# Adaptive-norm mixture of experts on one core: where the shared expert begins, who adds its residual, how fast the bit search is paced, and how the logits are made

## The reference, cut to what matters

```python
x = L0_attn_x                                  # (2, 2048, 128) float32, 4096 tokens
mod = (silu(L0_c) @ L0_wmod)                   # sa, ca, ga, sb, cb, gb; |ga|, |gb| at least 0.25
h = layernorm(x) * (1 + ca) + sa
x = x + ga * causal_mean(h)                    # running mean over the tokens of a sequence
h = layernorm(x) * (1 + cb) + sb
# ffn on xf = h as (4096, 128); E = 8 experts, F = 512
scores = softmax(xf @ gate_weight.T).T
vals, idx = top_k(scores.reshape(-1), 8192)    # over all experts and tokens together
gate = zeros((8, 4096)).at[idx // 4096, idx % 4096].add(vals)
y = gelu(xf @ W1[e] + b1[e]) @ W2[e] + b2[e]   # for each expert e
shared = gelu(xf @ Ws1 + bs1) @ Ws2 + bs2
out = x + gb * (sum over e of gate[e] * y[e] + shared)
```

## Time and profile before

| | |
|---|---|
| median of 3 runs | 421.06 us |
| profiled execution | 420.8 us, span 419.0 us |
| TensorE matmul busy | 293.0 us (70%) |
| VectorE | 181.8 us (43%) |
| ScalarE | 142.0 us (34%) |
| POOL (GpSimd) | 217.3 us (52%) |

### The profile page before, as it was taken

One profiled execution on the slowest core, in us unless ns is written; L12 is line 12 of the kernel. 1 busy time (PEld: TensorE's weight loads), 2 busy tenths in 40 slices (PEclk: granted clock), 3 DMA queues, 4 the chain that ended last, 5 costly groups with the idle time before them and its releaser, 6 DMA issues.

```text
span 419.0 us, 5097 instructions
## 1 busy us (share of the span) xinstructions
PE 293.0 (70%) x1182; PEld 165.6 (40%) x1182; DVE 181.8 (43%) x790; ACT 142.0 (34%) x228; POOL 217.3 (52%) x208
## 2 busy tenths in 40 slices
PE   1256676677899869799977878776798676895000
PEld 1144463444445446365544335444344443342000
DVE  0578989615666665534542343442243341121100
ACT  1014455465445432254423332233333223341000
POOL 0122523300111213655788778887778887756662
PEclk9999868657999996699989898898989889899555
DMA  8573322011011002935455554555544555323321
GB/s 241 144 196 96 106 77 75 25 52 13 0 39 39 25 27 55 280 85 166 84 114 121 122 110 62 102 122 120 118 91 88 99 122 118 69 26 30 31 27 18
DMA packets 50463, 37.04 MB, mean 88 GB/s; under 512 B 7879, under 2 KB 44542, under 8 KB 50430
## 3 DMA queue, kind: packets, MB, share of 16 engines
q0 software_dynamic: 13824, 14.46, 20.3%
q1 hardware_dynamic: 36368, 21.78, 18.3%
q10 hardware_dynamic: 238, 0.42, 0.3%
HBM read 24.70 MB, written 11.94 MB: 87 GB/s over the span
## 4 chain that ended last, share of the span: by engine, by line
issue 47%; POOL 31%; DMA 10%; PE 6%; DVE 2%; POOLq 1%; SPq 0%; ACT 0%; DVEq 0%
POOL out_dram L854 19%; POOL R L841 7%; DMA out_dram<-R,IDXB 4%; DMA R<-rows_scratch,IDXB 4%; PE U L942 2%; PE Y L962 2%; POOL SM L821 2%; POOL ACC L874 2%; DMA out_dram<-OUT 1%; DVE GJ L719 1%; PE R L907 1%; POOL SM L815 1%; DMA CST<-in_consts_dram 1%; PE R L1050 1%; POOL SM L823 1%
## 5 line engine op out<-in xcount | busy, mean ns | idle before, releaser
L854 POOL DMA_INDIRECT out_dram<-R,IDXB x72 | 113.2, 1572 | 34.6 <-issue 20.4
L841 POOL DMA_INDIRECT R<-rows_scratch,IDXB x72 | 70.2, 975 | 32.8 <-issue 19.1
L354 ACT ACTIVATE HF<-U,CB 128x512 f32<-128x512 f32 x72 | 49.5, 687 | 99.0 <-PE U L942 80.2
L962 PE MATMUL Y<-HF,WU 128*128 128x512 f32 x144 | 81.7, 655 | 0.0
L942 PE MATMUL U<-XT,WU 128*128 128x512 f32 x144 | 77.5, 620 | 0.7 <-issue 0.7
L907 PE MATMUL R<-CST,R 128*128 128x128 f32 x128 | 25.9, 337 | 41.2 <-DMA R<-rows_scratch,IDXB 36.7
L762 DVE SCALAR_TENSOR_TENSOR R<-R1b,GT,R 128x128 f32<-128x128 f32 x72 | 20.4, 344 | 66.3 <-PE R1b L907 37.7
L942 PEld LDWEIGHTS U<-XT,WU 128*128 128x128 f32 x144 | 29.6, 207 | 39.4 <-issue 39.4
L907 PEld LDWEIGHTS R<-CST,R 128*128 128x128 f32 x128 | 17.8, 168 | 54.5 <-DMA R<-rows_scratch,IDXB 47.5
L962 PEld LDWEIGHTS Y<-HF,WU 128*128 128x128 f32 x144 | 27.9, 206 | 27.0 <-issue 26.9
L874 POOL TENSOR_TENSOR ACC<-ACC,TMP 128x512 f32<-128x512 f32 x8 | 10.1, 1266 | 52.4 <-ACT TMP L404 52.4
(11 more groups left out here) (172 smaller groups left out, 403.7 us busy)
## 6 DMA issues: line engine op xcount, KB each, us to landing
WU<-in_L_ffn_W_dram SPq DMA_DIRECT2D x36, 256.0 KB
out_dram<-OUT SPq DMA_DIRECT2D x9, 256.0 KB, 2.4
R<-in_L_attn_x_dram SPq DMA_DIRECT2D x8, 256.0 KB, 3.5
INV<-in_inv_dram SPq DMA_DIRECT2D x8, 256.0 KB, 3.5
rows_scratch<-GBC SPq DMA_DIRECT2D x2, 1024.0 KB, 7.2
rows_scratch<-OUT SPq DMA_DIRECT2D x8, 256.0 KB, 3.2
R<-rows_scratch,IDXB POOLq DMA_INDIRECT x72
out_dram<-R,IDXB POOLq DMA_INDIRECT x72
```

The lines of the kernel that those rows point to most:

```text
L354: eng.activation(HF[:, g % RING, :], UB[g % 2][:, :], ACT.Gelu_apprx_tanh, bias=bias).then_inc(M["a_gelu"], 1)
L841: eng.indirect_dma_start(XG[:, v % XR, s, :], None, rows_dram, bass.IndirectOffsetOnAxis(ap=IDXB[:, v, s:s + 1], axis=0)).then_inc(M[f"ld_ ...
L854: eng.indirect_dma_start(out, bass.IndirectOffsetOnAxis(ap=IDXB[:, v, s:s + 1], axis=0), YO[:, v % 2, s, :], None, compute_op=ALU.add, bou ...
L962: eng.matmul(bank[:, :], down_weights(g), HF[:, g % RING, :], start=c == 0, stop=c == NC - 1).then_inc(M["pe_dn"], 1)
```

## The change

- The shared expert starts at step 28 (it was 44), beside the head's blocks 4 to 7. HEAD_STEPS is 15. TOPK_SLOT is 41 (44).
- PACE is 4: a bit in every half step, 30 bits in steps 43 to 57 (46 to 67). TIE0 is 58 (68), UNIT1 is 66 (76).
- T3 is copied from PSUM by ScalarE at h=6 to a token-major X2 in SBUF; second statistics and XN2 read X2. H2F, H2h keep h=10; T6 moves to h=13 and HT to h=14, the HT store too.
- The logits are four fp32 matmuls at h=12 with H2F as weights and the gate weights (8 columns) moving, in token order, straight into the bank LG. GWh, GWl, the three matmuls, the LR copy and the four transposes are gone.
- The scaled shared sum (TMP) alone is transposed, and VectorE adds X2 to it out of PSUM into SHO, which SP stores. POOL's add and ScalarE's closing copy are gone. VectorE's close stands between bits 2s and 2s + 1.
- The head has three PSUM banks for the whole time; Y0 and Y1 belong to the shared expert.

```diff
-HEAD_STEPS = 16
-UNIT0 = 44
+HEAD_STEPS = 15
+UNIT0 = 28
...
-PACE = 6
+PACE = 4
 UMIN = TOPK // BLK
-TOPK_SLOT = 4 * (NB - 1) + HEAD_STEPS
+TOPK_SLOT = 4 * (NB - 1) + 13
...
-    free = [(k, None) for k in range(5)]
+    free = [(k, None) for k in range(3)]
...
+        for b in range(NB):
+            h = s - 4 * b
+            if h == 4:
+                give(("t1", b), "v_ct", b + 1)
+                give(("t2", b), "v_x2", b + 1)
+            elif h == 6:
+                give(("t3", b), "a_x2", b + 1)
+            elif h == 10:
+                give(("t4", b), "a_h2f", b + 1)
+            elif h == 14:
+                give(("t6", b), "a_ht", b + 1)
...
-            give(("out", g // NC), "a_out", g // NC + 1)
+            give(("out", g // NC), "v_out", g // NC + 1)
...
-        ACC = sb("ACC", [P, S])
+        ACC = sb("ACC", [P, 2, BLK])
+        X2 = sb("X2", [P, NB, BLK])
+        SHO = sb("SHO", [P, 2, BLK])
...
-        GWh, GWl = sb("GWh", [P, E], F32R), sb("GWl", [P, E], F32R)
...
-        LR = R1[0:E, 5120:5632]
...
-        HB = RB + YB
+        HB = RB
...
-                    elif s - 4 * b == 13:
+                    elif s - 4 * b == 14:
                         eng.wait_ge(M["a_ht"], b + 1)
...
-                    eng.dma_start(dst, OUT[:, b % 2, :, :]).then_inc(M[f"st_out{b % 2}"], 16)
+                    eng.dma_start(dst, SHO[:, b % 2, :].rearrange("p (t c) -> p t c",
+                                                                  t=NT)).then_inc(M[f"st_out{b % 2}"], 16)
...
-                if h == 8:
+                if h == 6:
                     T3 = HB[BANK["t3", b][0]]
+                    eng.wait_ge(M["pe_t3"], b + 1)
+                    eng.activation(X2[:, b, :], T3[:, :], ACT.Copy).then_inc(M["a_x2"], 1)
+                elif h == 8:
+                    eng.wait_ge(M["a_x2"], b + 1)
                     eng.wait_ge(M["g_rs2"], b + 1)
                     if b:
                         eng.wait_ge(M["pe_t4"], b)
                     for t in range(NT):
-                        m = eng.activation(XN2[:, t, :], T3[:, t * P:(t + 1) * P], ACT.Identity,
+                        m = eng.activation(XN2[:, t, :], X2[:, b, t * P:(t + 1) * P], ACT.Identity,
                                            bias=RS[:, 1, 1, t:t + 1], scale=RS[:, 1, 0, t:t + 1])
                     m.then_inc(M["a_xn2"], 1)
                 elif h == 10:
...
-                elif h == 13:
+                elif h == 14:
                     T6 = HB[BANK["t6", b][0]]
...
-                elif h == 15:
-                    T5 = HB[BANK["t5", b][0]]
-                    eng.wait_ge(M["pe_lr"], b + 1)
-                    if b:
-                        eng.wait_ge(M["pe_lg"], b)
-                    eng.wait_ge(M["v_mod"], 1)
-                    eng.activation(LR, T5[0:E, :], ACT.Copy).then_inc(M["a_lr"], 1)
 
...
-                    eng.wait_ge(M["g_sh"], b - 1)
+                    eng.wait_ge(M["pe_out"], b - 1)
...
-            def close(b):
-                bank = HB[BANK["out", b][0]]
-                eng.wait_ge(M["pe_out"], b + 1)
-                if b >= 2:
-                    eng.wait_ge(M[f"st_out{b % 2}"], 16 * (b // 2))
-                else:
-                    eng.wait_ge(M[f"st_ht{b % 2}"], 16 * (NB // 2))
-                eng.activation(OUT[:, b % 2, :, :].rearrange("p t c -> p (t c)"), bank[:, :],
-                               ACT.Copy).then_inc(M["a_out"], 1)
...
-            eng.wait_ge(M["v_cols"], 1)
-            eng.tensor_copy(GWh[:, :], GWC).then_inc(M["v_gw"], 1)
-            eng.wait_ge(M["v_gw"], 1)
-            eng.tensor_tensor(GWl[:, :], GWC, GWh[:, :].bitcast(F32), ALU.subtract).then_inc(M["v_gw"], 1)
...
-                    eng.wait_ge(M["pe_t3"], b + 1)
-                    stats(b, 1, HB[BANK["t3", b][0]][:, :].rearrange("p (t c) -> p t c", t=NT), "v_ag2")
+                    eng.wait_ge(M["a_x2"], b + 1)
+                    stats(b, 1, X2[:, b, :].rearrange("p (t c) -> p t c", t=NT), "v_ag2")
...
+            def close(b):
+                bank = HB[BANK["out", b][0]]
+                eng.wait_ge(M["pe_out"], b + 1)
+                eng.wait_ge(M["a_x2"], b + 1)
+                if b >= 2:
+                    eng.wait_ge(M[f"st_out{b % 2}"], 16 * (b // 2))
+                eng.tensor_tensor(SHO[:, b % 2, :], bank[:, :], X2[:, b, :], ALU.add).then_inc(M["v_out"], 1)
...
-                g = on_step(s - 4)
-                if g is not None and g < GS0 and g % NC == NC - 1:
-                    b = g // NC
-                    eng.wait_ge(M["a_sh"], b + 1)
-                    eng.wait_ge(M["pe_t3"], b + 1)
-                    eng.tensor_tensor(acc_block(b), acc_block(b), TMP[:, b % 2, :], ALU.add).then_inc(M["g_sh"], 1)
...
-                    transposes(T3, lambda t: ACC[:, b * BLK + t * P:b * BLK + (t + 1) * P]).then_inc(M["pe_t3"], 1)
+                    transposes(T3, lambda t: ACC[:, b % 2, t * P:(t + 1) * P]).then_inc(M["pe_t3"], 1)
...
                 elif h == 12:
                     eng.wait_ge(M["a_h2f"], b + 1)
+                    eng.wait_ge(M["v_cols"], 1)
+                    for t in range(NT):
+                        j = (b * NT + t) * E
+                        m = eng.matmul(LG[:, j:j + E], H2F[:, t * P:(t + 1) * P], GWC, start=True, stop=True)
+                    m.then_inc(M["pe_lg"], 1)
+                elif h == 13:
+                    eng.wait_ge(M["a_h2f"], b + 1)
                     T6 = bank_free(("t6", b))
                     transposes(T6, lambda t: H2F[:, t * P:(t + 1) * P]).then_inc(M["pe_t6"], 1)
-                elif h == 14:
-                    hs, ls = H2h[:, b * BLK:(b + 1) * BLK], H2l[:, b * BLK:(b + 1) * BLK]
-                    eng.wait_ge(M["a_h2"], b + 1)
-                    eng.wait_ge(M["v_h2l"], b + 1)
-                    eng.wait_ge(M["v_gw"], 2)
-                    T5 = bank_free(("t5", b))
-                    eng.matmul(T5[0:E, :], GWh[:, :], hs, start=True, stop=False)
-                    eng.matmul(T5[0:E, :], GWh[:, :], ls, start=False, stop=False)
-                    eng.matmul(T5[0:E, :], GWl[:, :], hs, start=False, stop=True).then_inc(M["pe_lr"], 1)
-                elif h == 15:
-                    eng.wait_ge(M["a_lr"], b + 1)
-                    for t in range(NT):
-                        j = (b * NT + t) * E
-                        m = eng.transpose(LG[:, j:j + E], LR[:, t * P:(t + 1) * P], IDENT[0:E, 0:E])
-                    m.then_inc(M["pe_lg"], 1)
 
...
-                eng.wait_ge(M["g_sh"], b + 1)
+                eng.wait_ge(M["a_sh"], b + 1)
                 bank = bank_free(("out", b))
-                transposes(bank, lambda t: ACC[:, b * BLK + t * P:b * BLK + (t + 1) * P]).then_inc(M["pe_out"], 1)
+                transposes(bank, lambda t: TMP[:, b % 2, t * P:(t + 1) * P]).then_inc(M["pe_out"], 1)
```

More of the change, by code:

```diff
@@ L51 @@
 st_out0 st_out1 ld_xg0 ld_xg1 ld_xg2 ld_xg3 ld_xg4 st_sc0 st_sc1
-pe_cols pe_mod pe_gbc pe_t1 pe_t2 pe_t3 pe_t4 pe_t6 pe_lr pe_lg pe_up pe_dn pe_out pe_sum pe_tie pe_cum pe_dq
+pe_cols pe_mod pe_gbc pe_t1 pe_t2 pe_t3 pe_t4 pe_t6 pe_lg pe_up pe_dn pe_out pe_sum pe_tie pe_cum pe_dq
 pe_idx pe_xt pe_yt
-a_sil a_w a_xn2 a_h2f a_h2 a_ht a_lr a_gelu a_sh a_out a_exp a_dq a_xh a_ye
-v_cols v_gw v_mod v_gbd v_gbc v_zero v_wl v_st v_ag1 v_ag2 v_xn v_ct v_mt v_x2 v_h2l
+a_sil a_w a_xn2 a_h2f a_h2 a_ht a_gelu a_sh a_x2 a_exp a_dq a_xh a_ye
+v_cols v_mod v_gbd v_gbc v_zero v_wl v_st v_ag1 v_ag2 v_xn v_ct v_mt v_x2 v_h2l v_out
 v_tk v_sub v_sc v_cnt v_cand v_mask v_tie v_sel v_ds v_dq v_stc v_eid v_oh v_used v_hm v_idx v_ix v_gread
 v_cb1 v_cb2 v_gt v_yo
-g_tr g_half g_ve1 g_ve2 g_rs g_nm g_rs1 g_rs2 g_sh g_sct""".split()
+g_tr g_half g_ve1 g_ve2 g_rs g_nm g_rs1 g_rs2 g_sct""".split()
 def on_step(s):
@@ L85, in bank_table @@
     for s in range(UNIT1 + 8):
-        if s == UNIT0:
-            uses["Y0"], uses["Y1"] = (next(f for f in free if f[0] == k) for k in (3, 4))
-            free = [f for f in free if f[0] < 3]
+        for b in range(NB):
[9 more added lines that the diff above has]
+                give(("t6", b), "a_ht", b + 1)
         for b in range(NB):
@@ L245, in acc_block @@
         def acc_block(b):
-            return ACC[:, b * BLK:(b + 1) * BLK]
+            return ACC[:, b % 2, :]
         def down_weights(g):
@@ L376, in head @@
                         eng.wait_ge(M["pe_t6"], b)
+                        eng.wait_ge(M["pe_lg"], b)
                     eng.activation(H2F, T4[:, :], ACT.Identity, bias=SB2[:, n:n + 1],
@@ L450, in scalar @@
                     finish_shared(g // NC)
-                g = on_step(s - 6)
-                if g is not None and g < GS0 and g % NC == NC - 1:
-                    close(g // NC)
                 if s == TIE0 + 4:
@@ L623, in ties @@
                     bank = HB[BANK["tie"][0]]
+                    eng.wait_ge(M["pe_t6"], NB)
                     eng.wait_ge(M["pe_tie"], 1)
@@ L777, in vector @@
```

(5 more changed lines are left out.)

26 lines of the change are left out of this document (4 added, 22 removed).

## The result

The changed kernel takes **427.58 us** (median of 3 runs, 426.53 to 427.68) against 421.06: a ratio of 1.0157, with a 95% interval of 1.0113 to 1.0200. It is slower, by 6.5 us. The profiled execution took 427.68 (span 425.5; before 420.8 and 419.0).

The account below looks back on a forecast made before the run. POOL's indirect DMAs bound the kernel from the first scatter, so that scatter's start decides. Terms +10.1, +13.4, +0.2, -9.0, -1.25 and -6.5 sum to +6.95 on the profiled 420.8: forecast 427.8 us, range 416 to 436.

Parts of the forecast that it names:

- Head, +10.1: Head blocks up to the end of xn(6): it would end at 77.4 instead of 67.3, 10.1 us later.
- The loop: Head period from xn through transposes, logits, three ScalarE copies and statistics to next xn: 10.3 us summed, 10.0 taken.
- Shared stretch, +13.4: From the end of xn(6) to the last logits, beside the shared expert: 38 us instead of 24.6, 13.4 longer.
- Softmax +0.2: From the last logits to the first bit's sum: 6.4 us instead of 6.2.
- Bits -9.0: The 29 search intervals at 1.15 us plus four closes on VectorE: 37.6 us instead of 46.6.
- Ties -1.25: Ties and indices after the search: 1.25 us shorter, with POOL's adds gone from beside VectorE's work.
- Index to scatter -6.5: From first index to first scatter, 37.7 us before: 6.5 us shorter, with shared work ended before the units.
- After the scatter 0: From the first scatter to the end of the span, 219.1 us: nothing in the change touches it.
- (a): Head stays cheap, clock high or logits' weight loads hidden: loop 7.65, total 417.4 us, period below 8.5 decides; chance 0.20.
- (b): TensorE's clock stays low beside the shared expert, adding 11 us: total 438 us; chance 0.10.
- (c): Way from index to scatter gains nothing, TensorE cold at each gather wait: +6.5, total 434 us; chance 0.10.
- (d): Search bits stay at 1.5 us because VectorE's queue is the bound: +6, total 434 us; chance 0.05.

Follow-up runs that it names:

- 28 and 36: Changed kernel with second statistics reading T3 in PSUM, X2 copy out of the loop, and UNIT0 = 28 or 36: 413.31 and 413.20 us on one chip.
- late logits: Kernel with statistics from PSUM and UNIT0 = 28, with T6 at h=13 and the logits moved to h=14, behind T3: 419.19 us, 0.9957.
- early indices: Kernel with statistics from PSUM and UNIT0 = 36, with indices and gathers of units 3 and 4 moved ahead of the units: 416.11 us, 0.9883.

## Why the prediction was right

The forecast was 427.8, the time 427.58. By its own terms, each against what the two traces show:

- **Head, +10.1: measured +8.9** (xn(6) ends at 76.15, before 67.27). The loop is the one I wrote down, link by link; its period is 9.68, not 10.0 (my sum said 10.3). The logits hold TensorE's queue for 1.57, not 1.8, as the last of them overlaps the next group; the three copies take 1.96 to the statistics, not 2.15; statistics to xn is 1.27, not 1.5, as the old figure held a wait for POOL, whose L821 ended at 35.14.
- **Shared stretch, +13.4: measured +15.5** (40.1 us, not 38.0). The order of events was right. To the end of xn(7) it took 14.8 where I had 14.5; from there to the last logits 25.3 where I had 23.5. What I had at the fast level there was slow in part: logits 1.45 at 93.77, and at the end T4(7) started at 108.09 behind XN2, the down behind it took 1.92 and the group 1.06. How close the whole came is partly chance: in the kernel with PACE = 6, with the same queues, the first part took 12.7, the second 25.3 and the stretch 38.0.
- **Softmax +0.2: +0.1.**
- **Bits -9.0: -10.2.** The free interval is 1.15 as read from one pair of sums. The four closes cost 0.32 + 0.58 = 0.90 each for three and 0.32 for the last, whose second half falls behind the last sum; I took 1.05 for each of four. The add, for which no row stood, takes 0.69: between the 0.60 and 1.27 of the bounds, near the value taken.
- **Ties -1.25: -0.9. Index to scatter -6.5: -5.8.** POOL waited 3.54 and 0.94 for the indices of units 3 and 4, as described.
- **After the scatter 0: -1.1**, in POOL's waits for its own scatters to land (10.0 us against 11.3). Two profiled executions can't say whether that belongs to the change.

The terms before the scatter sum to +7.6 against +6.95. Four of the errors are of 0.7 to 2.1 us and partly cancel, and the -1.1 behind the scatter, which I had at nothing, takes off what was left over: the range was earned, the tenths were luck.

**The rivals.** (a) asked for a period under 8.5, with the clock high or the logits hidden. The groups took 1.06 and the logits 1.72, and doubling the logits moved the period by their whole length, so nothing of them was hidden. The period of 8.6 without the copy is not (a): there the groups are as slow, and the loop has lost a link. (b) asked for a slow clock in the whole shared stretch; most ups and downs ran fast and the stretch was 2.1 us too long, not 11. (c) asked for no gain on the way to the scatter and (d) for bits of 1.5; neither came. PACE = 6 in the changed kernel gave 1.5, so that length comes with the other pace and not from VectorE's own work in a bit.

**What the prediction didn't see** is that +10.1 and +13.4 are not two losses of one kind. Taking the overlap away returns 15 us at the logits and nothing at the end. Taking the copy away returns 15.5 at the logits and most of it at the end (12.8 us of the median). The copy in front of the statistics is what made the change slower than the kernel before; it is not all that the head lost, since T3 still stands behind the logits and the period is 8.6 against 7.88. What the early start of the shared expert is worth once the copy is out is open: 28 and 36 tie, and 44 was not run.

By the rule that I quoted from the Trainium skill ("TensorE: Matmul & The Clock Gate", Part 4), the head's groups would stay at the slow level. In the changed kernel they nearly all did: between 24 and 78 us groups of four took 1.05 to 1.12, and one pair (56.98) 1.76 where others took 1.97. It is no strict rule here, though. In the kernel with the statistics from PSUM, T1 and T2 of block 5 took 0.66 and 0.60 at 62.60 (and again at 62.82 when it was repeated), with no 512-column matmul in the head before them. And the runs don't show that the kind of work is the reason, since 1.6 us of 512-column matmuls per period left all but one pair at 1.06.

## What to carry to other kernels

When a copy is moved to an idle engine, ask who waits for it and what stands before it in that engine's queue: 0.58 us of copy behind two others, which wait for TensorE, cost 13 us here, and cost nothing once the reader took its operand from where it first appears. An overlap moves work, and is only as good as the place that it empties: the faster search was worth 6 us where the shared work had been begun early, and nothing in the old kernel, where it was left over. Look at SP's queue too: the last store of a stage can stand behind a load that waits for the next one. Before a chain is shortened, walk it once more as it will be: twice (late logits, early indices) the next wait was already standing there: a bank or a buffer held by the step that had been moved, or a queue whose tail it pushed back.

## What the runs showed of the hardware

- **The granted clock in the profile did not tell how long TensorE's small groups took.** The changed kernel with the pace of 6 happens to have a granted clock of 1.00 from 26 to 76 us, where the changed kernel has 0.66, 0.56 and 0.50 from 46 to 76. One of its windows (columns as above) and TensorE's timeline:

```profile
58.00:68.00 10.00, 6.36 (x31) 5.96 (x30) 7.05 (x25) 4.37 (x10) 2.92 (x6) 1.00 0.27 80
```

```profile
56.50 1.97 PE L891 MATMUL R<-CST,R 128*128 128x128 f32 x8 [3.55 <-DVE R L517]
58.26 1.72 PE L966 MATMUL LG<-COL,R 128*128 128x8 f32 x8
```

  A pair of groups takes 1.97 (one group 1.06) and the logits 1.72 at either reading, and the period is 9.7 in both. Later in the changed kernel, at 102.69 and 115.34, the logits take 0.95, and in the search a group takes 0.60. Durations, not the column, are to be gone by; why they disagree stays open.
- An fp32 matmul of 128x128 weights and 8 columns is two instructions; eight of them take 1.72 or 0.95 us. The row with 2 columns gave 0.22 an instruction, the same within a hundredth: 8 columns cost no more than 2.
- VectorE's L607 fell from 1.28 (L621 before) to 0.35 and L631 from 0.87 (L644 before) to 0.15 once no POOL add ran beside them; 29 of L594 (L608 before) went from 0.25 to 0.16 on average. The Trainium skill ("VectorE: DVE Perf Modes", Two Vector instructions with no wait between them) has VectorE's second read interface to SBUF as one that is shared with GpSimd. The L608 of 1.21 at 136.59, which reads two inputs from SBUF, ended within 0.03 us of the POOL add beside it (136.51, 1.26), which agrees. L607 reads one such input only, and no run here isolates its case.
- ScalarE's XN2 took 1.65 for four from SBUF and 1.50 for four from PSUM.
